# Expert rests in units of 32 rows: 28 full tiles and six mixed tiles of a 64-row couple and two 32-row singles

## What is computed

```python
def _L0_cond_ref(x, genre_embed, rms_w, wg_W, wg_b, gg_W, gg_b, W1, b1, W2, b2, W3, b3):
    xn = rms_w * (x * jax.lax.rsqrt(jnp.mean(x * x, axis=-1, keepdims=True) + EPS))
    gate = xn @ wg_W + wg_b + (genre_embed @ gg_W + gg_b)
    gate_w = jax.nn.softmax(gate, axis=-1)
    topk_w, topk_i = jax.lax.top_k(gate_w, 2)
    cw = jnp.sum(jax.nn.one_hot(topk_i, 8) * topk_w[..., None], axis=-2)
    h1 = jax.nn.relu(jnp.einsum('bsh,ehm->bsem', x, W1) + b1)      # 256 -> 512
    h2 = jax.nn.relu(jnp.einsum('bsem,emn->bsen', h1, W2) + b2)    # 512 -> 512
    out_e = jnp.einsum('bsen,enh->bseh', h2, W3) + b3              # 512 -> 256
    return jnp.einsum('bseh,bse->bsh', out_e, cw)
...
x = x + attn(cond(x, cond_256, ...), ...)
x = x + ffn(cond2(x, cond_256, ...), ...)
```

## Time and profile before

| | |
|---|---|
| median of 3 runs | 746.86 us |
| the runs | 746.86, 750.28, 746.14 us |
| the profiled execution, its own time | 744.04 us |
| its span, first to last instruction | 742.3 us |
| mean granted clock of TensorE | 0.989 |
| busy: PE, DVE, ACT, POOL | 712.1, 486.7, 287.5, 91.7 us |

### The profile page before, as it was taken

One profiled execution on the slowest core, in us unless ns is written; L12 is line 12 of the kernel. 1 busy time (PEld: TensorE's weight loads), 2 busy tenths in 40 slices (PEclk: granted clock), 3 DMA queues, 4 the chain that ended last, 5 costly groups with the idle time before them and its releaser, 6 DMA issues.

```text
span 742.3 us, 20364 instructions
## 1 busy us (share of the span) xinstructions
PE 712.1 (96%) x8218; PEld 612.2 (82%) x8218; DVE 486.7 (66%) x1036; ACT 287.5 (39%) x838; POOL 91.7 (12%) x102
## 2 busy tenths in 40 slices
PE   6289999999999999999999999999999999999997
PEld 2189999569999999978778878978888897888785
DVE  3856565644444444234777787787778778777867
ACT  3032121142212121254465446445544654564552
POOL 2131112511212101031101101110110111000000
PEclk9599999999999999999999999999999999999999
DMA  7789111217111102310001100100110010000000
GB/s 280 310 327 341 54 36 49 96 44 261 39 37 37 37 30 87 106 44 23 16 9 30 30 9 23 30 23 10 30 30 9 23 30 23 10 15 17 7 11 23
DMA packets 21259, 49.13 MB, mean 66 GB/s; under 512 B 3180, under 2 KB 14828, under 8 KB 18606
## 3 DMA queue, kind: packets, MB, share of 16 engines
q1 hardware_dynamic: 12112, 32.47, 12.1%
q0 software_dynamic: 3744, 10.49, 4.7%
q10 hardware_dynamic: 5309, 4.87, 2.0%
HBM read 41.00 MB, written 6.82 MB: 64 GB/s over the span
## 4 chain that ended last, share of the span: by engine, by line
PE 93%; DVE 3%; DMA 1%; ACT 1%; issue 1%; POOL 0%; SPq 0%; ACTq 0%; DVEq 0%; POOLq 0%
PE ps L790 16%; PE ps L891 15%; PE ps L760 8%; PE ps L824 8%; PE ps L917 8%; PE ps L976 7%; PE ps L942 4%; PE ps L992 3%; PE ps L935 2%; PE ps L967 2%; PE ps L1007 2%; PE ps L1069 2%; PE ps L1026 2%; PE ps L784 1%; PE ps L1039 1%; PE ps L739 1%
## 5 line engine op out<-in xcount | busy, mean ns | idle before, releaser
L891 PE MATMUL ps<-arena,l_weights 128*128 128x128 f32 x1024 | 125.9, 277 | 0.5 <-ACT arena L1462 0.5
L790 PE MATMUL ps<-h_t,w_now 128*128 128x128 f32 x1056 | 123.3, 275 | 0.0
L891 PEld LDWEIGHTS ps<-arena,l_weights 128*128 128x128 f32 x1024 | 119.3, 192 | 2.3 <-ACT arena L1462 1.0
L790 PEld LDWEIGHTS ps<-h_t,w_now 128*128 128x128 f32 x1056 | 120.5, 192 | 0.0
L1387 ACT ACTIVATE h_t<-ps,cols 128x128 f32<-128x128 f32 x132 | 37.6, 367 | 163.8 <-PE ps L760 148.8
L1918 DVE COPY w_now<-arena 128x2048 f32 x33 | 40.5, 1227 | 80.7 <-PE ps L790 77.1
L1468 ACT ACTIVATE arena<-ps,cols 128x128 f32<-128x128 f32 x256 | 74.0, 388 | 49.0 <-PE ps L891 49.0
L640 POOL DMA_INDIRECT arena<-expert_out,slot_of x32 | 33.0, 1031 | 323.9 <-DVE arena L1971 276.9
L760 PEld LDWEIGHTS ps<-xg_t,w_now 128*128 128x128 f32 x528 | 63.4, 192 | 4.9 <-ACT xg_t L1370 2.4
L760 PE MATMUL ps<-xg_t,w_now 128*128 128x128 f32 x528 | 65.0, 276 | 1.9 <-ACT xg_t L1370 1.9
L609 POOL DMA_INDIRECT xg<-in_x,slot_tok x36 | 42.5, 1181 | 186.7 <-PE ps L739 155.5
(11 more groups left out here) (365 smaller groups left out, 1094.3 us busy)
## 6 DMA issues: line engine op xcount, KB each, us to landing
arena<-in_experts SPq DMA_DIRECT2D x16, 1024.0 KB, 7.3
expert_out<-y ACTq DMA_DIRECT2D x36, 128.0 KB
arena<-in_x_t SPq DMA_DIRECT2D x2, 1024.0 KB, 6.2
arena<-in_x SPq DMA_DIRECT2D x16, 128.0 KB, 2.1
out<-arena SPq DMA_DIRECT2D x16, 128.0 KB, 1.7
b<-in_b SPq DMA_DIRECT2D x1, 1024.0 KB, 7.4
l_weights<-in_wq SPq DMA_DIRECT2D x1, 1024.0 KB, 5.0
l_weights<-in_wk SPq DMA_DIRECT2D x1, 1024.0 KB, 9.5
```

Source lines behind the costliest of these rows:

```text
L790: last = mm(ps[:, 2, m * P:(m + 1) * P], w2_now[:, k, m * P:(m + 1) * P], h1_t[j % 2][:, k, :], start=k == 0, stop=k == KM - 1)
L891: last = mm(ps[:, b, c * P:(c + 1) * P], wt[:, k, f:f + P], m_t[:, k, :], start=k == 0, stop=k == KH - 1)
```

## The change

The unit becomes 32 rows. An expert's rest is at most three units and is split into a couple, 64 rows, if there are two units or more, and a single, 32 rows, if the number is odd. A mixed tile now holds one couple in its lower 64 rows and two singles in the two quarters above (`UNIT_ROWS`). There are always 28 full tiles and six mixed ones, 34 in all, with the mixed ones at positions 13 to 18.

Layers 2 and 3 change in the same way as layer 1, which the diff shows. The copies of weights are made for the two singles alone (`COPIED = 2`). The couple's weights are streamed from `arena`, at an address that PE reads into a register two steps ahead (`load_couple`). The routing on DVE gets a third comparison (a row's place past the couple), a fourth segment of starts, and a few operations that place the last couples' chunks of 64 rows. POOL sets up the row numbers in three pieces.

```diff
-UNIT = 64
-UNITS = P // UNIT
-FULL = 33
+UNIT, COUPLE = 32, 64
+UNIT_ROWS = [slice(0, COUPLE), slice(COUPLE, COUPLE + UNIT), slice(COUPLE + UNIT, P)]
+COPIED = 2
+FULL = 28
...
+UNITS_IN_ALL = (TOPK * TOK + EXP * (UNIT - 1)) // UNIT
+MIXED = -(-max(UNITS_IN_ALL * UNIT - FULL * P, EXP * (COUPLE + UNIT)) // P)
...
+FIRST_MIXED = 13
+MIXED_POSITIONS = [FIRST_MIXED + n for n in range(MIXED)]
...
+            def load_couple(j):
+                if not mixed(j):
+                    return
+                if nth(j) == 0:
+                    pe.wait_ge(row_expert_set, 1)
+                e = pe.value_load(row_expert[0:1, nth(j):nth(j) + 1], min_val=0, max_val=EXP - 1)
+                couple_at[j] = pe.snap(e * E_SIZE)
...
                     for k in range(KH):
-                        for g in range(UNITS):
-                            part_ = slice(g * UNIT, (g + 1) * UNIT)
-                            last = mm(ps[part_, 0, :], xg_t[:, k, part_], w1_of[g][:, k, :],
-                                      start=k == 0, stop=k == KH - 1, tile_position=(0, g * UNIT))
+                        for g, part_ in enumerate(UNIT_ROWS):
+                            weight = w1_of[g - 1][:, k, :] if g else flat[:, bass.ds(couple_at[j] + W1_AT + k * MID, MID)]
+                            last = mm(ps[part_, 0, :], xg_t[:, k, part_], weight,
+                                      start=k == 0, stop=k == KH - 1, tile_position=(0, part_.start))
...
                 if exists(j, SLOT_TILES):
                     layer2(j)
+                load_couple(j + 2)
...
-                for g in range(UNITS):
-                    e = act.value_load(row_expert[g * UNIT:g * UNIT + 1, nth(j):nth(j) + 1], min_val=0, max_val=EXP - 1)
+                for g in range(COPIED):
+                    row_ = UNIT_ROWS[g + 1].start
+                    e = act.value_load(row_expert[row_:row_ + 1, nth(j):nth(j) + 1], min_val=0, max_val=EXP - 1)
...
+            step.go(tt(past_couple, past_full, couple_i, ALU.add))
...
+            step.go(tt(to_single, start_of[3], start_of[2], ALU.subtract))
+            step(tt(over_couple, rank, per_e(past_couple), ALU.is_ge))
...
+            step(tt(over_couple, over_couple, per_e(to_single), ALU.mult))
...
+            step(tt(over_full, over_full, over_couple, ALU.add))
...
-            step(dve.tensor_copy(slot_of[:, :, :], slot_f))
+            step(ts(past_split, slot_f, -float(SPLIT_AT), 0.0, ALU.add, ALU.max))
+            step.go(ts(shift_back, past_split, float(SPLIT * COUPLE), float(COUPLE - 2 * SPLIT * COUPLE), ALU.is_ge, ALU.mult))
+            step(ts(chunk_at, past_split, -COUPLE, None, ALU.bitwise_and))
+            step(tt(slot_f, slot_f, shift_back, ALU.add))
+            step(tt(slot_of[:, :, :], slot_f, chunk_at, ALU.add))
...
-                    for g in range(UNITS):
-                        part_ = slice(g * UNIT, (g + 1) * UNIT)
+                    for g, part_ in enumerate(UNIT_ROWS):
                         last = tt(y[part_, :], ps[part_, 4, 0:HID], b3[part_, bass.ds(experts_of[j][g] * HID, HID)], ALU.add)
```

More of the change, by code:

```diff
@@ L34 @@
 KM = MID // P
-UNIT = 64
-UNITS = P // UNIT
-FULL = 33
+UNIT, COUPLE = 32, 64
+UNIT_ROWS = [slice(0, COUPLE), slice(COUPLE, COUPLE + UNIT), slice(COUPLE + UNIT, P)]
+COPIED = 2
+FULL = 28
 def end_p2(t, n):
     return TT - 3 + 2 * (t - (TT - 3)) + n + 1
[L46 to L54, removed]
+UNITS_IN_ALL = (TOPK * TOK + EXP * (UNIT - 1)) // UNIT
+MIXED = -(-max(UNITS_IN_ALL * UNIT - FULL * P, EXP * (COUPLE + UNIT)) // P)
+SPLIT = EXP * UNIT // COUPLE
+COUPLES_AT, SPLIT_AT, SINGLES_AT = FULL * P, (FULL + MIXED - SPLIT) * P, FULL * P + EXP * COUPLE
 SLOT_TILES = FULL + MIXED
 LAST = SLOT_TILES - 1
-FIRST_MIXED = EXP + FULL - HOST
-LAST_MIXED = FIRST_MIXED + MIXED - 1
+FIRST_MIXED = 13
+MIXED_POSITIONS = [FIRST_MIXED + n for n in range(MIXED)]
+LAST_MIXED = MIXED_POSITIONS[-1]
 BIAS_BUFS = 2
@@ L121, in mixed, with out_block @@
 def mixed(p):
-    return FIRST_MIXED <= p <= LAST_MIXED
+    return p in MIXED_POSITIONS
 def nth(p):
-    return p - FIRST_MIXED if mixed(p) else p if p < FIRST_MIXED else p - MIXED
+    before = sum(at < p for at in MIXED_POSITIONS)
+    return before if mixed(p) else p - before
 def slot_tile(p):
[L134 to L138, removed]
+    return FULL + nth(p) if mixed(p) else nth(p)
+def out_block(p):
+    return p if p < EXP else EXP + nth(p) if mixed(p) else MIXED + nth(p)
 def later(t):
@@ L257, in build @@
         tot, scan_zero, incl, excl = (r(EXP, TT) for _ in range(4))
-        count_i, full_i, up_i = (r(EXP).bitcast(I32) for _ in range(3))
+        full_i, up_i = (r(EXP).bitcast(I32) for _ in range(2))
         past_first, past_full, to_first, to_full, to_rest, jump = (r(EXP) for _ in range(6))
-        seg, room, behind = r(3 * EXP + 1), r(1), r(EXP)
-        rank, over_first, over_full = (r(TT, EXP) for _ in range(3))
+        seg, room = r(4 * EXP + 1), r(2)
+        rests_i = r(2 * EXP).bitcast(I32)
+        past_couple, to_single = r(EXP), r(EXP)
+        rank, over_first, over_full, over_couple = (r(TT, EXP) for _ in range(4))
         picked = [over_first, over_full]
-        slot_f = r(TOPK, TT)
+        slot_f, shift_back = r(TOPK, TT), r(TOPK, TT)
+        past_split, chunk_at = r(TOPK, TT).bitcast(I32), r(TOPK, TT).bitcast(I32)
         slot_lo, slot_hi = r(TOPK, TT).bitcast(I32), r(TOPK, TT).bitcast(I32)
@@ L297, in build @@
         w1_b, w2_b = r(KH, MID), r(KM, MID)
-        w3_now = [r(KM, HID) for _ in range(UNITS)]
+        w3_of = [r(KM, HID) for _ in range(COPIED)]
         h1_rows, h2_rows = r(MID), r(MID)
@@ L600, in _ @@
             pool.wait_ge(mask_set, 2)
-            pool.iota(row_slot, pattern=[[P, MIXED]], base=FULL * P, channel_multiplier=1,
+            pool.iota(row_slot[:, 0:MIXED - SPLIT], pattern=[[P, MIXED - SPLIT]], base=COUPLES_AT, channel_multiplier=1,
                       allow_small_or_imprecise_dtypes=True).then_inc(row_slot_set, 1)
+            pool.wait_ge(row_slot_set, 1)
+            for upper in range(2):
+                pool.iota(row_slot[upper * COUPLE:(upper + 1) * COUPLE, MIXED - SPLIT:MIXED], pattern=[[COUPLE, SPLIT]],
+                          base=SPLIT_AT + upper * SPLIT * COUPLE, channel_multiplier=1,
+                          allow_small_or_imprecise_dtypes=True).then_inc(row_slot_set, 1)
             pool.wait_ge(ids_set, 1)
@@ L781, in layer2 @@
                     for k in range(KM):
[L782 to L785 removed]
+                        for g, part_ in enumerate(UNIT_ROWS):
+                            weight = w2_of[g - 1][:, k, :] if g else flat[:, bass.ds(couple_at[j] + W2_AT + k * MID, MID)]
+                            last = mm(ps[part_, 2, :], h1_t[j % 2][:, k, part_], weight,
+                                      start=k == 0, stop=k == KM - 1, tile_position=(0, part_.start))
                     last.then_inc(l2_ps, 1)
@@ L807, in layer3 @@
                     for k in range(KM):
-                        for g in range(UNITS):
-                            part_ = slice(g * UNIT, (g + 1) * UNIT)
-                            last = mm(ps[part_, 4, 0:HID], h2_t[j % 2][:, k, part_], w3_now[g][:, k, :],
-                                      start=k == 0, stop=k == KM - 1, tile_position=(0, g * UNIT))
+                        for g, part_ in enumerate(UNIT_ROWS):
+                            weight = w3_of[g - 1][:, k, :] if g else flat[:, bass.ds(couple_at[j] + W3_AT + k * HID, HID)]
+                            last = mm(ps[part_, 4, 0:HID], h2_t[j % 2][:, k, part_], weight,
+                                      start=k == 0, stop=k == KM - 1, tile_position=(0, part_.start))
                     last.then_inc(y_ps, 1)
@@ L1878, in unit_expert @@
             def unit_expert(j, g):
-                return dve.value_load(row_expert[g * UNIT:g * UNIT + 1, nth(j):nth(j) + 1], min_val=0, max_val=EXP - 1)
+                row_ = UNIT_ROWS[g].start
+                return dve.value_load(row_expert[row_:row_ + 1, nth(j):nth(j) + 1], min_val=0, max_val=EXP - 1)
             def take_w1(j):
-                if j == EXP:
+                if nth(j) == EXP and not mixed(j):
                     dve.wait_ge(experts_set, 2)
@@ L1910, in take_w2 @@
                 if mixed(j):
-                    for g in range(UNITS):
-                        at = dve.snap(experts_of[j][g] * E_SIZE + W2_AT)
+                    for g in range(COPIED):
+                        at = dve.snap(experts_of[j][g + 1] * E_SIZE + W2_AT)
                         last = dve.tensor_copy(w2_of[g][:, :, :].rearrange("p k n -> p (k n)"), arena[:, bass.ds(at, KM * MID)])
```

70 lines of the change are left out of this document (38 added, 32 removed).

## The result

| | before | changed |
|---|---|---|
| median | 746.88 us | 792.03 us |
| lowest and highest of 4 runs | 746.14, 750.28 | 791.85, 792.48 |
| the profiled execution, its own time | 744.04 us | 791.85 us |
| its span | 742.3 us | 790.1 us |
| mean granted clock of TensorE | 0.989 | 0.983 |

The ratio is 1.0601, with a 95% interval of 1.0583 to 1.0619. The forecast was 795.3 us; its own range (787 to 811) holds the time.

The account below looks back on a forecast made before the run. PE was taken as the bound, busy for 96% of the span. 744.0 - 36.5 + 26.4 + 56.8 + 1.8 = 792.5 us, plus 2.8 to the median: 795.3 us; 787 to 811, or 736 to 811 with the abreast case.

Parts of the forecast that it names:

- Part one: Experts' stage on PE: five fewer full tiles save 36.5 us, three more mixed tiles cost 26.4 us, 10.1 us less.
- Part two: Mixed tiles on PE: couple and singles run one after the other, with changes of shape; +56.8 us over six tiles.
- The rival's page: Source for the rival that unequal shapes run abreast in mixed tiles: 738.5 us (736 to 743), chance 0.21.
- The term: Mixed tiles on PE: extra passes and 17 more shape changes at 0.15 us, 9.46 us per tile, +56.8 us for six.
- Part three: Routing on DVE, in front of PE's long wait for the slots: new operations count in full, +1.8 us (1.4 to 2.5).
- The parts at no cost: Address registers, weight copies, bias pieces and gathers, weight loads and row tables lie beside PE's work: no time added.
- The last step: From profiled execution to median: 2.8 us added to 792.5 us, giving 795.3 us.

Follow-up runs that it names:

- four quarters: The changed kernel with every mixed matmul of 32 columns, the couple multiplied in two pieces (same work size, not its true values): 738.31 us, ratio 0.9871 to before.
- one kind: The changed kernel's 28 full and six mixed tiles, but each mixed tile holds only two couples or only four singles: 739.23 us, ratio 0.9899 to before.
- four times 32: The kernel before with both units of its three mixed tiles multiplied as two pieces of 32 columns each: 747.33 us, ratio 0.9999.

## Why the prediction was right, and where its terms were off

**Part one** held: a full step is 7.30 us in the changed kernel too.

```profile
305.72 1.95 PE L780 MATMUL ps<-xg_t,w_now 128*128 128x128 f32 x16
...
313.02 1.95 PE L780 MATMUL ps<-xg_t,w_now 128*128 128x128 f32 x16
```

**Part two** held, and with it the choice between the shapes abreast and one after the other. The singles start 1.01 us after the couple in layers 1 and 2 and 0.57 in layer 3, where 0.86 + 0.15 and 0.43 + 0.15 were forecast. It was right to rest this on the weight loads: before, a load waited at a change of shape where the columns were in use; in the changed kernel it waits as long, 0.81 us, where they are free. The Trainium skill, TensorEngine Tiling (Array Packing), section Tiling Modes, has it so: to change the mode drains the engine. The runs agree, down to a drain between disjoint columns, which no row of before could show: 1.01 us from one shape's start to the next. They show the order, not the circuit's reason. The rival's page (the Trainium skill, TensorE: Matmul & The Clock Gate, the section on the array as 16 blocks) isn't contradicted, but its concurrency reaches here only among matmuls of one shape.

The term was sized a little high. With 0.432 us a pass, a change measures (1.99 - 4 x 0.432) / 2 = 0.13 us, and (1.13 - 4 x 0.216) / 2 = 0.13 in layer 3, not 0.15. A mixed tile costs 17.83 - 8.72 = 9.11 us more, not 9.46, and six 54.7, not 56.8. With parts one and two that makes -36.5 + 26.4 + 54.7 = 44.6 us from the first mixed layer to attention; the trace has 44.44.

**Part three** held: PE's wait grew from 10.4 to 12.1 us, by 1.7 for 1.8 forecast. The remap's four operations more take 0.7 us of it, as the kernel without them shows (11.4).

**The parts at no cost** cost nothing in this kernel: no idle mark in a mixed step, and the terms above leave no room for registers or copies. One small cost lies hidden in its long steps, though: where the mixed steps are short again, PE waits 1.28 us (four quarters) and 1.18 us (one kind) for DVE at the first mixed tile, a wait that the kernel before doesn't have.

**The last step was off**, the 2.8 us between the median and the profiled execution of before, which the forecast carried over. The changed kernel's four runs lie within 0.6 us and its profiled one 0.2 below their median. Of the 2.8 us, 1.8 lie at one place in the profiled execution of before. The rows are POOL's first gather of x, PE's turning of its rows and ScalarE's copy of them, in the kernel before and then in the one with four times 32:

```profile
34.43 1.10 POOL L609 DMA_INDIRECT xg<-in_x,slot_tok  x1 [29.01 <-DVE slot_tok L1857]
38.06 0.39 PE L739 MATMUL ps<-ident,xg 128*128 128x128 f32 x2
38.54 0.37 ACT L1370 COPY xg_t<-ps 128x256 f32<-128x256 f32 x1 [15.63 <-PE ps L739]
```

```profile
34.56 1.10 POOL L610 DMA_INDIRECT xg<-in_x,slot_tok  x1 [29.14 <-DVE slot_tok L1855]
37.98 0.39 PE L740 MATMUL ps<-ident,xg 128*128 128x128 f32 x2
40.52 0.37 ACT L1368 COPY xg_t<-ps 128x256 f32<-128x256 f32 x1 [17.47 <-remote]
```

From issue to copy it is 4.11 us before, 5.96 there, 5.88 in the changed kernel, and 5.79 to 5.96 in all seven kernels profiled beside it. It isn't the gather's transfer that was faster: in all eight, its 48 packets (0.13 MB) are moved within 2.8 us of the issue. Nor is it the recorded start of the turning, 38.06 and 37.98; only the copy behind it comes 0.48 us after that start before and 2.54 us there. What held the copy in the seven no row shows; the cause stays open. So 1.8 of the 2.8 us were the luck of that one execution, at a place on the path. That the other executions of before took the usual time is argued from the kernel with four times 32, whose set-up is the same; it wasn't seen. The sum against the profiled execution therefore had to gain these 1.8, and the median nothing on top. Corrected so: 744.0 - 36.5 + 26.4 + 54.7 + 1.7 + 1.8 = 792.1 us. Two small differences of single executions, 0.9 us more behind attention's start and 1.0 less ahead of the slots, cancel. Of the 3.3 us that the forecast lay too high, 2.1 are thus the price of the changes of shape, and 1.0 is what was carried over beyond the 1.8.

**A reading that fell.** Next to the slots, the 40 matmuls that keep PE busy took 2.60 us before and 3.59 in the changed kernel. The granted clock rose from 0.50 (1.2 GHz) to 1.00 (2.4 GHz) while PE worked on them, later in the changed kernel: in mean it was 0.91 over the block before and 0.63 after. One could put 1.0 us of the loss there. In the kernel with four times 32 the block takes 2.41 us, at a granted clock of 1.00, and the first copy still comes 5.96 us after the gather's issue. So it isn't the block's length that sets that copy, and no row shows that the half clock cost time there.

## What to carry to other kernels

Matmuls in different columns of the array ran side by side only when their tiles had the same shape: pack leftovers so that each tile holds one shape, and let the shape differ from tile to tile instead. A smaller unit that saves tiles (10.1 us in all by the sum, 7.4 measured with tiles of one kind) isn't worth a mixture that costs each mixed tile a second set of passes (9.1 us). And before adding "median less profiled execution" to a forecast, look for the place in the trace where that execution differs from others of the same work.

## What was unexpected

The spread at the first gather: 4.11 us in one execution against 5.79 to 5.96 in seven, from its issue to the copy of its turned rows, though its packets took the same time in all. And how little finer pieces cost by themselves: four matmuls of 32 columns in place of two of 64 (747.33 against 747.68 us) were free.
